# Result stores of the routed last layer, issued inside the loop over block quads

## The chip, the cores and the metric

The kernel runs on one core of a Trainium2 chip. The metric is the device time of one launch in microseconds. The kernel before took 2792.13 us, the median of three runs (2788.15 to 2796.69).

## What is computed

Four layers on x of shape 4 x 2048 x 256, each added to x after a layer norm: a linear attention with random features, a soft mixture of experts, a causal attention with rotary positions, and a mixture of 32 experts with the two best experts for each token. The change lies in the last layer:

```python
x = x + _L1_attn_ref(...)
x = x + _L1_ffn_ref(_layernorm(x, axis=-1), router_w, expert_weights)

# _L1_ffn_ref
logits = einsum('bsh,eh->bse', x, router_w)
rw = softmax(logits).reshape(T, E)
vals, idx = top_k(rw, 2)
w_masked = zeros_like(rw).at[arange(T)[:, None], idx].set(vals)
out = sum over experts e of (x_flat * w_masked[:, e:e+1]) @ expert_weights[e]
```

## The kernel before

X holds all tokens in SBUF: 64 tiles of 128 tokens, 256 values each, 64 KB a partition. The last stage, `tail`, first finishes the attention (output projection, added to X) and finds for each token its two experts and its places in a buffer in DRAM in which the tokens lie sorted by expert (`dest`). The tiles are dealt with in three groups (`TAIL`): tiles 0 to 15, 16 to 47 and 48 to 63. Each group has its own buffer of blocks of 128 rows: 64, 96 and 64 blocks (`BLOCKS`), 224 together. A block belongs to one expert. Four blocks are a quad: 56 quads, q = 0 to 55, of which 0 to 15 belong to the first group, 16 to 39 to the second, 40 to 55 to the third. Two blocks are a pair: 112 pairs, j = 0 to 111.

For each group the steps are:

- **GpSimd** scatters the tokens of a tile to their two places, two indirect DMAs a tile (L2054).
- **SyncE** loads a quad of sorted rows into one of four buffers `xin` (`load`, L2003) and stores a quad of results from one of two buffers `yout` (`keep_y`, L2008). Its program is a list written out in order: four loads, then for each q the store of quad q and the load of quad q + 4, and after the last quad the sixteen result stores (L2015 to L2017), each of four tiles of X (512 KB, in rows of 1 KB) to the output. Store f waits for the additions of tiles 4f to 4f + 3.
- **TensorE** transposes a pair (L2366) and multiplies it by its expert's weights (L2417). It is three pairs ahead with the transposes: the first pair of quad q + 4 is transposed just ahead of the multiplication of pair 2q + 5.
- **ScalarE** copies the transposed pair (L2283) and the products into `yout` (L2290). `keep_y(q)` waits for the product of pair 2q + 1.
- **GpSimd** gathers the two result rows of each token, two indirect DMAs a tile (L2065). The first gather of a group waits until all quads of the group have landed in DRAM; every tile waits for the additions of the tile four before it, since there are four slots.
- **VectorE** adds the two weighted rows to X, two operations a tile (L2268, L2270), and raises `added`.

SyncE executes its list strictly in order, so what waits in it holds back what stands behind.

Of the kernel before, what the change touches and what calls it, by code (L numbers as in the profile page):

```python
# [15 lines left out]
NT = B * TPB  # L16
# [1876 lines left out]
def tail(nc, mem, io, keep, st):  # L1893

    X, mean, rstd, ident = keep["X"], keep["mean"], keep["rstd"], keep["ident"]
# [45 lines left out]
    xc_ready, multiplied, y_ready, restored, added, stored = (mem.sem(n) for n in (  # L1941
        "xc_ready", "multiplied", "y_ready", "restored", "added", "stored"))
# [18 lines left out]
    ov = io["out"].rearrange("b (q n p) d -> (b q) p n d", n=4, p=P)  # L1961
# [7 lines left out]
    def wait_sent(eng, g):  # L1969

        t0, tiles = TAIL[g]
        for s in range(NO):
            eng.wait_ge(sent[s], 32 * len(range(s, t0 + tiles, NO)))

    with nc.Block() as block:
        @block.sync
        def _(sp):
            sp.sem_inc(a_loaded[0], 16)
            for c in range(1, NT // 4):
                if c >= 2:  # L1980
                    sp.wait_ge(projected, 2 * (c - 2) + 2)
                if c == NT // 4 - 1:
                    sp.wait_ge(last_stored, 64)
                sp.dma_start(ay[c % 2][:, :, :], ao[c // 4, :, c % 4 * 512:(c % 4 + 1) * 512].rearrange("(c p) n -> p c n", p=P)).then_inc(a_loaded[c % 2], 16)
                if c >= 1:
                    for a in range(DC):
                        e = slice(2 * c - 2, 2 * c)
                        sp.dma_start(W[:, a, e, :], io["we"][e, a * P:(a + 1) * P, :].rearrange("e p d -> p e d")).then_inc(w_loaded, 16)
                if c == 2:
                    sp.wait_ge(last_divided, 1)  # L1990
                    for h in range(4):
                        sp.dma_start(keep["ao"][B * G - 1, h, :, 3 * 512:4 * 512],
                                     keep["aT1"][32 * h + h % 2 * HD:32 * h + h % 2 * HD + HD, :]).then_inc(last_stored, 16)
            for a in range(DC):
                sp.dma_start(W[:, a, 30:32, :], io["we"][30:32, a * P:(a + 1) * P, :].rearrange("e p d -> p e d")).then_inc(w_loaded, 16)

            def load(q):
                g = group_of[q * NB]
                if q * NB == base[g]:
                    wait_sent(sp, g)  # L2000
                if q >= NX:
                    sp.wait_ge(turned, NP + (q - NX + 1) * NB // 2)
                sp.dma_start(xin[q % NX][:, :, :], xgv[g][q - base[g] // NB]).then_inc(x_in[q % NX], 16)  # L2003

            def keep_y(q):
                g = group_of[q * NB]
                sp.wait_ge(y_ready, (q + 1) * NB // 2)
                sp.dma_start(ygv[g][q - base[g] // NB], yout[q % NY][:, :, :]).then_inc(y_out[q % NY], 16)  # L2008
            for q in range(NX):
                load(q)  # L2010
            for q in range(NQ):
                keep_y(q)
                if q + NX < NQ:
                    load(q + NX)
            for q in range(NT // 4):  # L2015
                sp.wait_ge(added, q * 4 + 4)
                sp.dma_start(ov[q], X[:, q * 4:q * 4 + 4, :]).then_inc(stored, 16)  # L2017
            sp.wait_ge(stored, 16 * (NT // 4))

        @block.gpsimd  # L2020
# [252 lines left out]
        def _(act):  # L2273
# [32 lines left out]
            def restore(t):  # L2306
                for g, (t0, _) in enumerate(TAIL):
                    if t == t0:
                        wait_sent(act, g)
                s.activation(X[:, t, :], X[:, t, :], ACT.Identity, bias=mean[:, t:t + 1]).then_inc(restored, 1)  # L2310
# [233 lines left out]
```

## Time and profile before

| what | value |
|---|---|
| median of three runs | 2792.13 us |
| the profiled execution's own time | 2787.93 us |
| its span, first to last instruction | 2786.1 us |
| PE, ACT, DVE, POOL busy | 89%, 64%, 56%, 26% |
| mean granted TensorE clock | 0.956 of full speed |
| DMA traffic over the span | 308.9 MB, mean 111 GB/s |

The profile covers one execution. Its span is 1.8 us shorter than its own time, and its own time is 4.2 us below the median, within the spread of the three runs. The shares are means over all stages; the change touches the last 155 us alone, where the loop over quads ends at 2734 us and the last gathers and stores end at 2786 us.

### The profile page before, as it was taken

What the parts mean: (1) busy time and instruction counts of PE and PEld (TensorE: products, weight loads), DVE (VectorE), ACT (ScalarE), POOL (GpSimd) and SP (SyncE); (2) the same over time, 40 slices, a digit from 0 to 9 for tenths busy, and PEclk for the clock granted to TensorE, in tenths of its full rate; (3) what the DMA queues carried; (4) which work ended last, traced back from release to release, by engine and by line L of the source; (5) the groups of instructions that cost most, each with busy time, mean ns of one, the idle gap of its engine ahead of it and who ended that gap; (6) DMA issues with size and microseconds to landing.
All of it is one profiled execution on the core that took longest, in us unless ns stands there. A gap on an engine that the chain in (4) does not pass through costs nothing. (4 is left out here: it accounts for less than half of the span.)

```text
span 2786.1 us, 64193 instructions
## 1 busy us (share of the span) xinstructions
PE 2475.4 (89%) x25127; PEld 1442.7 (52%) x25131; DVE 1569.5 (56%) x2607; ACT 1793.5 (64%) x2682; POOL 736.8 (26%) x1006
## 2 busy tenths in 40 slices
PE   7888888887788989987999999999999998897992
PEld 4555555554677766653334333333333337776771
DVE  4767768577766557755554445555454437840223
ACT  3443535344455434546999999999999992465540
POOL 3203021030000016861211122221211120475566
PEclk9999999999899999988999999999999999899996
DMA  7800000000200004474766756666766605587887
GB/s 252 287 32 2 1 1 1 1 1 1 48 1 1 1 12 147 138 164 114 127 124 114 123 105 105 120 127 116 119 122 117 113 10 154 173 289 244 279 291 258
DMA packets 252048, 308.90 MB, mean 111 GB/s; under 512 B 100592, under 2 KB 180208, under 8 KB 251632
## 3 DMA queue, kind: packets, MB, share of 16 engines
q1 hardware_dynamic: 237392, 269.49, 41.0%
q0 software_dynamic: 12288, 33.57, 3.4%
q8 instruction: 200, 3.28, 0.5%
q10 hardware_dynamic: 2080, 1.84, 0.2%
q14 instruction: 88, 0.72, 0.1%
HBM read 157.23 MB, written 147.59 MB: 109 GB/s over the span
## 5 line engine op out<-in xcount | busy, mean ns | idle before, releaser
L1816 ACT ACTIVATE at_PT<-at_pS 128x1024 f32<-128x1024 f32 (+2 forms) x1152 | 1002.3, 1256 | 9.1 <-PE at_pS L1843 8.9
L1670 POOL TENSOR_SCALAR_AFFINE_SELECT at_PT<-at_PT 128x256 f32<-128x256 f32 (+1 forms) x384 | 197.5, 523 | 820.3 <-ACT at_PT L1816 819.8
L1843 PE MATMUL at_pS<-hd_QT,hd_KT 99*32 99x512 bf16 (+3 forms) x5120 | 316.9, 351 | 7.8 <-DVE at_QT L1788 5.1
L1843 PE MATMUL at_pS<-at_QT,at_KT 99*32 99x512 bf16 (+3 forms) x5120 | 318.1, 348 | 2.2 <-issue 0.7
L1767 DVE COPY md_y<-at_pO 128x512 f32<-128x512 f32 x64 | 44.2, 691 | 474.7 <-PE at_pO L1861 469.9
L1861 PE MATMUL at_pO<-at_PT,at_V 128*32 128x512 f32 (+3 forms) x2560 | 289.7, 529 | 0.3 <-POOL at_PT L1670 0.3
L1861 PE MATMUL at_pO<-at_PT,hd_V 128*32 128x512 f32 (+3 forms) x2560 | 286.8, 529 | 0.6 <-issue 0.6
L1843 PEld LDWEIGHTS at_pS<-hd_QT,hd_KT 99*32 99x32 bf16 x5120 | 111.4, 95 | 268.8 <-ACT at_PT L1816 174.1
L1843 PEld LDWEIGHTS at_pS<-at_QT,at_KT 99*32 99x32 bf16 x5120 | 114.6, 95 | 257.3 <-ACT at_PT L1816 169.0
L457 ACT ACTIVATE la_ft<-la_ft 128x1024 f32<-128x1024 f32 x128 | 135.2, 1056 | 161.5 <-DVE la_ft L280 161.2
L2417 PE MATMUL tl_bank<-tl_W,tl_xT 128*128 x896 | 225.6, 390 | 14.5 <-issue 13.3
L273 DVE TENSOR_REDUCE la_mx<-la_pW 128x16 f32<-128x1024 f32 x128 | 155.0, 1211 | 87.5 <-PE la_pW L571 87.5
L514 POOL TENSOR_SCALAR la_ft<-la_ft 128x1024 f32<-128x1024 f32 x64 | 66.8, 1045 | 465.2 <-ACT la_ft L457 465.2
L2417 PEld LDWEIGHTS tl_bank<-tl_W,tl_xT 128*128 128x128 f32 x896 | 156.8, 191 | 55.4 <-issue 40.2
L1336 POOL TENSOR_TENSOR qk_rqk<-qk_xc,qk_xs 128x256 f32<-128x256 f32 x64 | 54.1, 845 | 470.7 <-DVE qk_xs L1262 463.7
L2054 POOL DMA_INDIRECT rows_in<-all_X,all_dest x128 | 123.9, 968 | 165.0 <-DVE all_dest L2205 90.8
L280 DVE TENSOR_TENSOR la_ft<-la_pW,la_mx 128x1024 f32<-128x1024 f32 x128 | 156.8, 1225 | 10.0 <-issue 0.5
L2283 ACT ACTIVATE tl_xT<-tl_bank 128x512 f32<-128x512 f32 x144 | 85.1, 591 | 102.7 <-PE tl_bank L2366 102.3
L1437 PE MATMUL qk_pQK<-fr_W,qk_zT 128*128 128x512 f32 x256 | 128.2, 625 | 18.4 <-ACT qk_zT L1373 18.4
L553 PE MATMUL la_R<-la_zT,la_qkv_w 128*128 128x512 f32 x256 | 124.4, 632 | 21.7 <-ACT la_zT L406 21.7
L2268 DVE SCALAR_TENSOR_TENSOR all_X<-md_ay,all_wt,all_X 128x256 f32<-128x256 f32 x32 | 15.6, 486 | 181.3 <-DMA md_ay<-rows_out,all_dest 181.0
L1593 DVE RECIPROCAL md_y<-md_y 128x512 f32<-128x512 f32 x32 | 107.3, 3353 | 2.7 <-issue 0.4
(376 smaller groups left out, 4297.1 us busy)
## 6 DMA issues: line engine op xcount, KB each, us to landing
tl_xin<-rows_in SPq DMA_DIRECT2D x56, 512.0 KB, 5.6
score_terms<-at_parts SPq DMA_DIRECT2D x60, 384.0 KB, 6.2
rows_in<-la_zeros SPq DMA_DIRECT2D x8, 2048.0 KB, 7.9
rotated_qk<-qk_qkT SPq DMA_DIRECT2D x16, 1024.0 KB, 4.5
at_qk<-rotated_qk SPq DMA_DIRECT2D x60, 256.0 KB, 4.3
rows_out<-md_y SPq DMA_DIRECT2D x28, 512.0 KB
rows_out<-tl_yout SPq DMA_DIRECT2D x28, 512.0 KB, 3.8
rows_in<-la_zeros SPq DMA_DIRECT2D x4, 3072.0 KB, 10.8
```

What stands on the lines that cost most here:

```text
L273: v.tensor_reduce(mx[s % 2][:, :], src, AX, ALU.max)
L280: v.tensor_tensor(ft[s % 4][:, :].rearrange("p (h m) -> p h m", h=H), src, mx[s % 2][:, :].unsqueeze(2).broadcast_to([P, H, M]), ALU.subtr ...
L457: sc.activation(ft[s % 4][:, :], ft[s % 4][:, :], ACT.Exp, scale=0.25).then_inc(exp_done, 1)
L553: last = mm(out[:, :], W[:, a, col:col + P], zT[:, a, :], start=(a == 0), stop=(a == DC - 1))
L1437: last = mm(pQK[f % 2][:, :], zT[f][:, c, :], W[:, c, 0:2 * D], start=(c == 0), stop=(c == DC - 1))
L1593: v.reciprocal(out[:, :], out[:, :])
L1670: nc.gpsimd.affine_select(out=d, in_=d, compare_op=ALU.is_ge, fill=0.0, base=0, pattern=of, channel_multiplier=-1).then_inc(masked, 1)
L1816: nc.scalar.activation(PT[u % 6][:, 0:banks, 0:width], pS[u % 3][:, 0:banks, 0:width], ACT.Exp, scale=HD ** -0.5).then_inc(exp_done, 1)
L1843: last = mm(pS[u % 3][r:r + 32, b, col:col + 512 - off], KT[par][0:KS, h, kb * P + r:kb * P + r + 32], QT[par][0:KS, h, c * 512 + off:(c + ...
L1861: last = mm(pO[c % 2][32 * h:32 * h + 32, off:512], V[par][:, kb, VCOL[h]:VCOL[h] + 32], PT[u % 6][:, b, col:col + 512 - off], start=(kb = ...
L2054: g_.indirect_dma_start(out=keep["xg"][g], out_offset=bass.IndirectOffsetOnAxis(ap=dest[:, k, t:t + 1], axis=0), in_=X[:, t, :], in_offset ...
L2417: last = mm(pP[j % 3][:, w * D:(w + 1) * D].unsqueeze(1), xT[(NP + j) % 4][:, w, a, :], W[:, a, ds(e, 1), :], start=(a == 0), stop=(a == D ...
```

## The change

The last loop is split. The stores of tiles 0 to 43 (f = 0 to 10) are issued within the loop over quads, one at every second quad from q = 35 to q = 55, behind `keep_y(q)` and `load(q + 4)`; f = 11 to 15 follow after the loop. Every store keeps its wait. Nothing else is changed: the other engines' instructions are the same.

```diff
+            def store(f):
+                sp.wait_ge(added, f * 4 + 4)
+                sp.dma_start(ov[f], X[:, f * 4:f * 4 + 4, :]).then_inc(stored, 16)
             for q in range(NQ):
                 keep_y(q)
                 if q + NX < NQ:
                     load(q + NX)
-            for q in range(NT // 4):
-                sp.wait_ge(added, q * 4 + 4)
-                sp.dma_start(ov[q], X[:, q * 4:q * 4 + 4, :]).then_inc(stored, 16)
+                if q >= 35 and (q - 35) % 2 == 0:
+                    store((q - 35) // 2)
+            for f in range(11, NT // 4):
+                store(f)
             sp.wait_ge(stored, 16 * (NT // 4))
```

The list of SyncE, first at quads 35 to 37, before. `rows_out` is the store of a quad (from `tl_yout` for odd q, from `md_y` for even q), `tl_xin` the load four quads ahead, `out_dram` a result store.

```order
 L2008 DMA rows_out<-tl_yout 128x1024
 L2003 DMA tl_xin<-rows_in 128x1024
-L2008 DMA rows_out<-md_y 128x1024
-L2003 DMA tl_xin<-rows_in 128x1024
-L2008 DMA rows_out<-tl_yout 128x1024
-L2003 DMA tl_xin<-rows_in 128x1024
```

And with the change, at the same place:

```order
+L2014 DMA out_dram<-all_X 128x4x256
+L2008 DMA rows_out<-md_y 128x1024
+L2003 DMA tl_xin<-rows_in 128x1024
+L2008 DMA rows_out<-tl_yout 128x1024
+L2003 DMA tl_xin<-rows_in 128x1024
+L2014 DMA out_dram<-all_X 128x4x256
```

A result store now stands behind the load of each odd quad, ahead of the next even quad's store and load.

The end of SyncE's list, from quad 51 on. Before, the four last quad stores and then all sixteen result stores:

```order
-L2008 DMA rows_out<-md_y 128x1024
-L2008 DMA rows_out<-tl_yout 128x1024
-L2008 DMA rows_out<-md_y 128x1024
-L2008 DMA rows_out<-tl_yout 128x1024
-L2017 DMA out_dram<-all_X 128x4x256 x16
```

With the change:

```order
+L2014 DMA out_dram<-all_X 128x4x256
+L2008 DMA rows_out<-md_y 128x1024
+L2008 DMA rows_out<-tl_yout 128x1024
+L2014 DMA out_dram<-all_X 128x4x256
+L2008 DMA rows_out<-md_y 128x1024
+L2008 DMA rows_out<-tl_yout 128x1024
+L2014 DMA out_dram<-all_X 128x4x256 x6
```

Eight result stores stand ahead of quad 51's store, one each behind quads 51 and 53, and six (f = 10 to 15) behind quad 55.

## Rows read from the trace of the kernel before

**Rows 1.** Chain that ended last, 2630 us to the end: start us, us, what.

```profile
2668.80 6.63 DMA tl_xin<-rows_in
...
2675.48 0.66 PE tl_bank L2366 x4
2676.13 0.46 issue
2676.59 2.02 PE tl_bank L2417 x8
...
2679.05 1.73 PE tl_bank L2417 x8
...
2683.96 6.85 DMA tl_xin<-rows_in
...
2715.43 6.15 DMA tl_xin<-rows_in
...
2778.58 2.72 DMA tl_ay<-rows_out,all_dest
```

**Rows 2.** GpSimd in order of time, the gathers (idle before, and what ended it).

```profile
2656.48 0.94 POOL L2065 DMA_INDIRECT md_ay<-rows_out,all_dest  x1 [25.35 <-DMA rows_out<-tl_yout]
...
2738.14 0.95 POOL L2065 DMA_INDIRECT md_ay<-rows_out,all_dest  x1 [0.30 <-issue]
...
2760.83 0.94 POOL L2065 DMA_INDIRECT md_ay<-rows_out,all_dest  x1 [1.16 <-issue]
...
2778.58 0.94 POOL L2065 DMA_INDIRECT tl_ay<-rows_out,all_dest  x1 [0.30 <-issue]
```

**Rows 3.** SyncE's queue in order of time: quads 39, 53, 55, and the sixteen stores.

```profile
2652.91 0.32 SPq L2008 DMA_DIRECT2D rows_out<-tl_yout  x1
...
2725.44 0.32 SPq L2008 DMA_DIRECT2D rows_out<-tl_yout  x1
...
2734.28 0.32 SPq L2008 DMA_DIRECT2D rows_out<-tl_yout  x1
2734.65 48.54 SPq L2017 DMA_DIRECT2D out_dram<-all_X  x16
```

**Rows 4.** VectorE in order of time: second additions of tiles 39 and 63.

```profile
2722.59 0.48 DVE L2270 SCALAR_TENSOR_TENSOR all_X<-tl_ay,all_wt,all_X 128x256 f32<-128x256 f32 x1
...
2782.30 0.48 DVE L2270 SCALAR_TENSOR_TENSOR all_X<-tl_ay,all_wt,all_X 128x256 f32<-128x256 f32 x1 [0.43 <-issue]
```

**Rows 5.** Stretches: busy time by engine; last: TensorE clock, DMA share, GB/s.

```profile
2634.00:2664.00 30.00, 28.18 (x146) 22.45 (x145) 2.00 (x4) 13.24 (x24) 5.69 (x7) 1.00 0.68 237
2664.00:2724.00 60.00, 54.27 (x279) 42.92 (x278) 22.91 (x48) 25.51 (x46) 45.88 (x47) 1.00 0.89 305
...
2744.00:2754.00 10.00, 0.00 (x0) 0.00 (x0) 3.01 (x7) 0.00 (x0) 7.55 (x9) 0.50 1.06 385
```

**Rows 6.** L2003, loads issued 2640 to 2720 us (quads 36 to 51).

```profile
L2003 SPq DMA_DIRECT2D tl_xin<-rows_in x16: 320/432/1252, 2640.0 to 2715.4; - x16
...
DMA to landing us min/median/max: 4.1/5.6/6.6
```

**Rows 7.** The load issued at quad 48, alone.

```profile
L2003 SPq DMA_DIRECT2D tl_xin<-rows_in x1: 436/436/436, 2699.8 to 2699.8; - x1
...
DMA to landing us min/median/max: 5.9/5.9/5.9
```

**Rows 8.** L2017, the sixteen result stores: duration ns, then landing us.

```profile
L2017 SPq DMA_DIRECT2D out_dram<-all_X x16: 372/1444/2088, 2734.6 to 2782.8; - x16
...
DMA to landing us min/median/max: 2.9/7.6/9.6
```

**Rows 9.** What TensorE waited for, 2634 to 2735 us: total us, times, longest.

```profile
PE tl_bank L2417 <- issue: 6.0, 13, 0.7
PE tl_bank L2366 <- DMA tl_xin<-rows_in: 1.9, 4, 0.8
```

## The prediction

> **What bounds the kernel now.** I read the chain that ended last first, from 2630 us on, because the change touches nothing earlier. It runs through three kinds of work: TensorE's pairs, now and then a load of sorted rows that TensorE waited for, and from the last quad store on GpSimd's gathers [rows 1]. The reader is to see that no result store is in it except the very last. Then GpSimd's order of time [rows 2]. Its gathers for tiles 16 to 63 start at 2656.48 us, when quad 39 has landed in DRAM, and go on almost without a gap to 2778.58 us: 96 gathers of some 1.25 us each (0.94 busy, 0.30 between). The third group's 32 gathers may start when quad 55 has landed. So two things hold the end at once: GpSimd's own pitch from 2656.48 us on, and the quad store issued at 2734.28 us [rows 3]. How close the second is: quad 39's store was issued at 2652.91 us and GpSimd started 3.57 us later; the same 3.57 us behind 2734.28 us is 2737.85 us, and GpSimd came to the third group at 2738.14 us. The slack is 0.3 us. Whatever delays the product of quad 55 by more than that delays the end one for one.
>
> **What the burst at the end costs now.** The sixteen result stores stand from 2734.65 us to 2783.2 us in SyncE's queue [rows 3]. The first eleven are ready when the loop ends (their tiles' additions are done), and they fill the DMA engines: 385 GB/s and a share of 1.06 from 2744 to 2754 us [rows 5], 1.44 us of the queue for each and 7.6 us to landing in the median [rows 8]. But the last store waits for the additions of tile 63, which end at 2782.78 us [rows 4], and lands 2.9 us behind its issue [rows 8], long after the burst is gone. The burst can cost only what it does to the gathers beside it: the 32 gathers of the third group are issued over 41.4 us (2738.14 to 2779.52) where 32 at 1.25 us would take 40.0; one gap of 1.16 us instead of 0.30 stands at 2760.83 us [rows 2].
>
> **The change, part by part.**
>
> *Eleven stores leave the end.* Of those 1.4 us I take the one gap, 1.16 - 0.30 = 0.9 us, as the gain, since gathers that take over 1 us are found elsewhere too. Bounds: a gain of 1.4 us and, if the gap has another cause, 0. The last five stores stay as they are; f = 10 stays right behind quad 55, where the burst began already.
>
> *Eleven waits on `added` enter SyncE's list.* Behind each are the next quad's store and load. The first four (tiles 0 to 15) were added before 2638 us and wait for nothing later than that. From f = 4 on the additions run close ahead of the quads. The smallest slack of these is that of f = 9: tile 39 is done at 2723.07 us, and SyncE is through with the store of quad 53 at 2725.76 us, 2.7 us later [rows 3, 4]. A wait that overran would hold back nothing at once, since the next quad's store comes 5.09 us after this one (16 quads from 2652.91 to 2734.28 us [rows 3]). So additions have to be later by 6 us and more before this wait costs. I cost it at nothing; the cover is the pace of GpSimd, which the change leaves.
>
> *Eleven transfers of 512 KB enter the loop.* This is the term that decides. A store stands behind the load of its odd quad in the same queue, so the next even quad's store and load start behind it. Per quad the loop now moves 0.52 MB of products, 0.52 MB of sorted rows and some 0.53 MB of gathers (305 GB/s times 5.09 us is 1.55 MB in all) [rows 5]. At the highest rate that the trace shows, 385 GB/s, this takes 4.0 us of the 5.09 us, so 1.1 us is free; one store more takes 0.52 MB / 385 GB/s = 1.4 us, with the gathers that go on beside it 1.8 us. The backlog that meets the next load is between 1.4 - 1.1 = 0.3 and 1.8 - 1.1 = 0.7 us. I take 0.7 us, since rate and share are at their ceiling for a whole quad only in the burst.
>
> Which loads does it meet? Those issued at quads 36 to 50, even ones. In the stretch up to 2664 us there are hardly gathers, 237 GB/s in the mean [rows 5], and the free time covers the store: 0 for f = 0 and 1, so quad 39 and GpSimd's start at 2656.48 us stay. There remain the six loads issued at quads 40, 42, 44, 46, 48 and 50. How late may a load be? The sixteen loads of quads 36 to 51 take 5.6 us in the median, 4.1 at least [rows 6]; those that the chain passes through landed after 6.63, 6.85 and 6.15 us [rows 1], while one of 5.9 us is not in it [rows 7]. I put the limit at 6.0 us. One of the six, of 6.63 us (quad 42), is over it already and passes on the whole 0.7 us; quad 40's meets few gathers and passes on nothing; I take four at the median, which go from 5.6 to 6.3 us, 0.3 over the limit each: 0.7 + 4 x 0.3 = 1.9 us. A TensorE that waited for its rows starts again slowly: 0.46 us of issue and 2.02 instead of 1.73 us for the next eight multiplications [rows 1], 0.75 us. Four loads would newly do that, 3.0 us; but 13 such pauses, 6.0 us, are there already against only four waits for loads [rows 9], so a new one will often stand in for an old one. I take half, 1.5 us (0 and 3.0 us stay as bounds). Sum: TensorE ends 1.9 + 1.5 = 3.4 us later.
>
> *Sum.* 3.4 - 0.3 (slack of quad 55) - 0.9 (burst) = +2.2 us on 2787.93 us, the profiled execution's own time: 2790.1 us. The runs' median is 4.2 us above that execution; the same 2.2 us on 2792.13 us gives **2794.3 us**. Measurements of this kernel tell some 0.3%, 8.4 us, from no change, so this is "same".
>
> *The upper end.* If each of the six loads is later by what one more store costs the queue in the burst, 1.44 us [rows 8], five at the median go to 7.0 us, 1.0 over the limit each, and quad 42's passes on 1.4: 6.4 us, with five restarts 3.8 us; no gain from the burst: 6.4 + 3.8 - 0.3 = +9.9 us, 2802 us.
>
> **The rivals.**
>
> *A, hidden altogether.* The backlog drains in the 5 us between quads, or the late loads fall together with pauses that are there. Then GpSimd's pitch alone sets the end and the burst's share is won: -0.9, at best -1.4 us, 2791 us. For it: TensorE waited only 1.9 us for loads in 100 us [rows 9]. Against it: the loads that it did wait for make up the chain [rows 1].
>
> *B, slower.* The DMA engines are full in the loop, the queue doesn't drain between one store and the next, and the backlog grows from quad to quad. Place: the ten loads issued at quads 42 to 51. Price: if they take what the stores of the burst took, 7.6 us [rows 8], each is 1.6 us over the limit; 1.6 us of that is there already (0.6, 0.85 and 0.15 us), so 16 - 1.6 = 14.4 us, and seven new restarts of 0.75 us, 5.3 us: +19 us, 2811 us. It decides from where the traffic asked for reaches the ceiling. Asked for from 2664 to 2724 us are 305 GB/s x 60 us = 18.3 MB and six stores, 3.1 MB: 21.4 MB or 357 GB/s. Against it: 385 GB/s are shown, 7% more [rows 5]. For it: that rate was reached with a full queue, in which each transfer waits long.
> The Trainium skill's page "DMA: Bandwidth & Descriptors", section "Where 436 GB/s comes from", speaks for this rival: it says that transfers between HBM and SBUF are bound on the HBM side at about 358 GB/s a core. By that ceiling the loop would be exactly full and rival B would be the likeliest. The trace's 385 GB/s over 10 us disagrees with it on this chip, so I leave B as a rival.
>
> *C, SyncE is held by a store's wait.* Gathers delayed by the traffic push the additions 6 us back (slack 2.7 us plus most of a quad), the quad store behind comes late, and with it the end. Gathers would have to take over 10 us, none here is near that. If it came, each us past the 6 would cost 1 us: 2796 to 2803 us.
>
> *D, faster by over 0.3%.* I find no mechanism, since the gathers' own pitch holds from 2656.48 us on, and the stores cost at most 1.4 us. Only the spread of the medians could show it.
>
> **How the numbers follow.** My forecast (a net slip of 0 to 8 us) 0.57; A 0.25; B 0.08; C 0.02; the remainder, a slip of 8 to 12 us by larger backlogs than I take, 0.03; D 0.05. The three runs before spread by -4.0 and +4.6 us around their median. The range takes A less most of that spread, 2791 - 4, and goes up to the upper end of the forecast: 2787 to 2802 us. Faster 0.05, same 0.82, slower 0.13.
>
> **What would show it.** In the changed kernel's profile: result stores of the loop issued without idle time ahead of the next quad store; loads issued at even quads from 42 on landing 0.3 to 0.7 us later than those at odd ones, 6 us and more; TensorE's wait for loads from 2634 us up from 1.9 us to 3 or 4 us; quad 55's store at 2736 to 2739 us instead of 2734.28; and the first gather of the third group waiting for `rows_out`. The gap ahead of the gather at 2760 us gone, and 385 GB/s found nowhere for long. I am wrong if quad 55's store is where it was (A), if loads take over 7 us at odd quads too (B), or if SyncE waits for VectorE between quads (C).

## The result and the profile after

The changed kernel takes 2801.41 us (median of nine runs, 2798.57 to 2808.07), the kernel before, on the same chip, 2792.11 us (nine runs). The ratio is 1.0037, with a 95% interval of 1.0025 to 1.0048: 9.3 us slower. Forecast was no change, +2.2 us.

The profiled execution has a span of 2799.8 us, 13.7 us above that of the profile before. That is more than the 9.3 us between the medians, because the execution profiled before lay 4.2 us below its median and this one at its median. Where the 13.7 us come from is read from SyncE's queue and GpSimd. SyncE's queue in order of time (start us, us, engine line op), around quads 39, 43 and 55:

```profile
2657.56 0.32 SPq L2008 DMA_DIRECT2D rows_out<-tl_yout  x1
...
2680.81 0.32 SPq L2008 DMA_DIRECT2D rows_out<-tl_yout  x1
2681.17 0.43 SPq L2003 DMA_DIRECT2D tl_xin<-rows_in  x1
2681.65 0.77 SPq L2014 DMA_DIRECT2D out_dram<-all_X  x1
2687.37 0.32 SPq L2008 DMA_DIRECT2D rows_out<-md_y  x1
...
2692.33 0.32 SPq L2008 DMA_DIRECT2D rows_out<-tl_yout  x1
...
2749.78 0.32 SPq L2008 DMA_DIRECT2D rows_out<-tl_yout  x1
```

Quad 35's store is at 2635.80 us (2633.53 us before): these 2.3 us arose before the first early store, so the change did not make them. From quad 35 to quad 55 the loop takes 113.98 us, before it took 100.75 us: **+13.2 us**. And the time goes in one place: from an odd quad's store to the next even one's it is now 6.5 us in the median (6.56 us above, 2680.81 to 2687.37), from an even one's to the next odd one's 5.0 us (4.96 us above). Before, they were 5.0 and 4.9 us. The early store stands in the long interval.

GpSimd, start of the second and of the third group:

```profile
2661.26 0.95 POOL L2070 DMA_INDIRECT md_ay<-rows_out,all_dest  x1 [28.16 <-DMA rows_out<-tl_yout]
...
2753.18 0.94 POOL L2070 DMA_INDIRECT md_ay<-rows_out,all_dest  x1 [10.30 <-issue]
```

The third group starts at 2753.18 us, after 10.3 us without work, 3.4 us behind quad 55's store. Before, GpSimd came to it without a wait [rows 2]. From there to the end it is 46.6 us (2753.18 to 2799.8), before 48.0 us: the burst at the end had cost 1.3 us. So 2.3 + 13.2 - 0.5 (slack and landing of quad 55: GpSimd started 3.9 us behind that store before, 3.4 us now) - 1.3 = 13.7 us.

What TensorE waited for between the stores of quads 35 and 55 (us in total, times, longest):

```profile
PE tl_bank L2422 <- issue: 17.7, 25, 1.2
PE tl_bank L2371 <- DMA tl_xin<-rows_in: 1.2, 2, 0.8
```

The stretches that answer to [rows 5] (last: TensorE clock, DMA share, GB/s):

```profile
2634.00:2664.00 30.00, 25.46 (x129) 20.15 (x130) 0.97 (x2) 11.38 (x21) 2.13 (x3) 1.00 0.78 256
2664.00:2724.00 60.00, 48.94 (x242) 38.50 (x242) 20.86 (x44) 22.25 (x42) 45.68 (x48) 0.97 0.96 321
```

The DMA engines carry 321 instead of 305 GB/s, and TensorE is busy for 48.9 instead of 54.3 us of the 60. The waits answer to [rows 9]. The waits for loads, on which the forecast rested, went down from 1.9 to 1.2 us. What grew, by 11.7 us, are the pauses ahead of multiplications in which the engine waits for nothing that the profile shows. These pauses are the greater part of the 13.2 us, but not all of it. The same 463 instructions of TensorE between the stores of quads 35 and 55 are also busy for longer, before and with the change:

```profile
2633.53:2734.28 100.75, 91.98 (x463) 72.09 (x462) 28.91 (x60) 42.69 (x77) 59.24 (x61) 1.00 0.80 275
2635.80:2749.78 113.98, 94.36 (x463) 73.54 (x462) 31.58 (x66) 42.36 (x77) 62.44 (x64) 0.99 0.87 291
```

TensorE's idle time grew by 10.9 us (the 11.7 us of pauses, less what the waits for loads fell) and its busy time by 2.4 us. A part of the latter goes with the clock: the granted clock was 0.90 from 2717 to 2722 us, where the engine was busy for 2.9 of 5 us in a wait for rows and two pauses, and 0.76 in the next 5 us; in the profile before it was 1.00 in both. TensorE's order of time behind the store of quad 43 shows where they stand:

```profile
2682.15 0.60 PE L2371 MATMUL tl_bank<-all_ident,tl_xin 128*128 128x128 f32 x4
2683.24 1.13 PE L2422 MATMUL tl_bank<-tl_W,tl_xT 128*128 x4 [0.48 <-issue]
2685.59 1.13 PE L2422 MATMUL tl_bank<-tl_W,tl_xT 128*128 x4 [1.23 <-issue]
2686.55 0.60 PE L2371 MATMUL tl_bank<-all_ident,tl_xin 128*128 128x128 f32 x4
```

A pause ahead of the first four multiplications of a pair, and one in its middle, ahead of the second four. Nothing changes hands in the middle of a pair: both blocks' rows and the result's bank are ready. But there is one instruction there that is no matrix work. `multiply` reads each block's expert from SBUF into a register (`pe.value_load(which[...])`), once ahead of every four multiplications, since the address of the weights depends on it. All 25 pauses stand ahead of such a group of multiplications. That became the theory.

A rival would be that TensorE waited for its own program to be fetched. The traces speak against it: between the stores of quads 35 and 55 the DMA queues marked "instruction" carry 9 packets before and 9 with the change, while the pauses go from 13 to 25, more than one for each packet.

### The profile page after: what moved, and what is told of

Read it like the earlier page. It is cut to its first block and busy times, and to the rows that moved or that the text cites. A ratio compares the mean times of both kernels' runs of the same rounds, so it can differ in the third digit from the quotient of the medians.

```text
span 2799.8 us, 64193 instructions
## 1 busy us (share of the span) xinstructions
PE 2474.7 (88%) x25127; PEld 1444.0 (52%) x25131; DVE 1570.8 (56%) x2607; ACT 1792.9 (64%) x2682; POOL 737.4 (26%) x1006
```

## The experiments

**Theory R**: the pauses are these register loads, which take longer while the DMA engines carry the early store. **Theory L**, the prediction's: sorted rows land late.

The runs came to several chips, and these are of two kinds. Chips of kind A run the kernel before in 2790 to 2792 us: that of the result and those numbered 3 and 9. Chips of kind B take 2838 to 2844 us: those numbered 6, 7 and 11. "Chip A" and "chip B" stand for a chip of the kind in what follows. A profile of the kernel before on chip B (before_again) shows the added time in the loop over quads: 344.8 us from quad 0 to quad 55, on chip A 290.3 us, part of it in stalls in which TensorE advances by one or two instructions with some 2 us between them. Why was not found. Ratios are to runs of the kernel before on the same chip, and can differ by up to 3 us from the quotient of the two medians shown. Two versions that ran on different chips are compared by their ratios, which is weaker than a comparison on one chip.

| run | chip | median us | before us | ratio, 95% interval | pauses behind odd quads | behind even quads |
|---|---|---|---|---|---|---|
| before (profile) | A | | | | 2.4 us | 2.9 us |
| changed | A | 2801.41 | 2792.11 | 1.0037 [1.0025, 1.0048] | 12.3 | 2.1 |
| even_too | A 3 | 2807.21 | 2790.45 | 1.0060 [1.0045, 1.0075] | 11.2 | 3.3 |
| even_only | A 9 | 2797.21 | 2791.14 | 1.0018 [1.0005, 1.0032] | 2.3 | 8.8 |
| sbuf_all | A 3 | 2802.47 | 2790.45 | 1.0052 [1.0034, 1.0069] | 7.5 | 2.4 |
| even_const | A 3 | 2783.81 | 2790.45 | 0.9976 [0.9964, 0.9987] | 0 | 0 |
| multi8_after | A 3 | 2782.24 | 2790.45 | 0.9973 [0.9961, 0.9985] | 0 | 0 |
| multi8_before_again | A 9 | 2783.26 | 2791.14 | 0.9966 [0.9951, 0.9981] | 0 | 0 |
| before_again (one run) | B 11 | 2845.18 | 2843.89 | | 3.1 | 3.2 |
| after_again | B 11 | 2848.14 | 2843.89 | 1.0013 [1.0001, 1.0024] | 7.5 | 4.9 |
| const_before | B 6 | 2823.59 | 2838.30 | 0.9946 [0.9930, 0.9962] | 0.3 | 0 |
| const_after | B 6 | 2825.31 | 2838.30 | 0.9945 [0.9925, 0.9965] | 0 | 0 |
| rows_4k | B 6 | 2841.66 | 2838.30 | 1.0012 [1.0000, 1.0025] | 8.7 | 3.6 |
| extra_loads | B 6 | 2842.53 | 2838.30 | 1.0012 [1.0002, 1.0021] | 4.7 | 1.7 |
| sbuf_copy | B 7 | 2844.26 | 2843.38 | 1.0003 [0.9989, 1.0016] | 3.4 | 4.7 |
| dram_copy | B 7 | 2842.87 | 2843.38 | 1.0001 [0.9990, 1.0012] | 5.0 | 2.1 |
| part16 | B 7 | 2843.00 | 2843.38 | 1.0003 [0.9990, 1.0016] | 6.0 | 4.6 |
| multi4_before | B 11 | 2831.40 | 2843.89 | 0.9965 [0.9952, 0.9978] | 0 | 0 |
| multi4_after | B 11 | 2835.47 | 2843.89 | 0.9972 [0.9963, 0.9982] | 0 | 0 |
| multi8_before | B 7 | 2833.43 | 2843.38 | 0.9962 [0.9950, 0.9975] | 0.8 | 0 |

The last two columns are sums over one profiled execution: TensorE's pauses ("issue") ahead of multiplications of the loop, in the nine intervals from an odd quad's store (35 to 53) to the next even one's and in the eight from an even one's (36 to 52) to the next odd one's, quads 41 to 43 left out in all of them because of chip B's stall there. One execution each, so differences of a few us between such sums are not told from chance; even_only's profile is of one of its slowest executions (2803.98 us, its median is 2797.21 us).

**Without the register loads.** Both kernels with the experts as constants. The blocks are multiplied by other experts' weights than they should be, so the result is not that of the layer; the work is the same.

```diff
-                    e = pe.value_load(which[0:1, 2 * j + w:2 * j + w + 1], min_val=0, max_val=E1 - 1)
+                    e = (2 * j + w) % E1
...
-                        last = mm(pP[j % 3][:, w * D:(w + 1) * D].unsqueeze(1), xT[(NP + j) % 4][:, w, a, :], W[:, a, ds(e, 1), :], start=(a == 0), stop=(a == DC - 1))
+                        last = mm(pP[j % 3][:, w * D:(w + 1) * D].unsqueeze(1), xT[(NP + j) % 4][:, w, a, :], W[:, a, e:e + 1, :], start=(a == 0), stop=(a == DC - 1))
```

const_before: 

> The kernel before, with the expert of each block written into TensorE's program as a constant (block number modulo 32) instead of read from SBUF into a register by an instruction of TensorE; the products are those of other experts, the work is the same. Theory R (TensorE's pauses, called issue in its waits, are its register loads from SBUF, which take longer while DMA engines read SBUF): the pauses between the multiplications, 2.3 + 3.3 + 1.3 + 4.7 = 11.6 us from 2521 to 2734 us, go to under 3 us, and the whole is 4 to 8 us faster than before. Theory L (the prediction's: loads of sorted rows land too late): pauses stay within 1 us of 11.6 us, time within 2 us of before.

const_after: 

> The changed kernel with the same constants in place of the register loads. Theory R: the pauses from 2634 us on, 17.6 us in the changed kernel, go to under 4 us, and the time is within 3 us of const_before, where the changed kernel is 9.3 us above the kernel before. Theory L: the difference to const_before stays 8 to 11 us, with the waits for tl_xin making it up.

Waits of TensorE between the stores of quads 35 and 55, const_before:

```profile
PE tl_bank L2366 <- DMA tl_xin<-rows_in: 12.7, 8, 3.5
PE tl_bank L2366 <- issue: 8.4, 5, 2.3
...
PE tl_bank L2417 <- issue: 1.5, 2, 1.2
```

and the same of the kernel before on that chip:

```profile
PE tl_bank L2417 <- issue: 17.0, 16, 4.0
PE tl_bank L2366 <- DMA tl_xin<-rows_in: 8.0, 4, 3.1
```

The pauses ahead of multiplications are gone, 16 of them become 2, and in const_after there is none. What is left of chip B's stall now stands ahead of transposes (L2366, 8.4 us; 13.5 us in 7 places in const_after). The time is 15 us below before, and the changed kernel and the kernel before have the same ratio. Theory L's mark, 8 to 11 us between the two, is missed. The gain is larger than expected (4 to 8 us). On this chip alone the second half says less than it seems, because the change costs little there:

> The changed kernel once more, on the chip of this call. Theory R and theory L: 1.002 to 1.005 times before, as on the first chip. If it is within 0.15% of before here, the loss of the change depends on the chip and the four experiments of the second chip have to be read by their pauses, not by their times.

> The kernel before once more, for a profile on the chip of this call: the chip of the first four experiments ran it in 2838.3 us, 46 us above the first chip. Both theories: the time of its own runs; the pauses of TensorE from quad 35 to quad 55 and its waits for rows on this chip are the base for the three runs beside it.

after_again is 1.0013: the loss is 4 us on chip B, 9 us on chip A, just below the range expected. The pauses behind odd quads rise there too, from 3.1 to 7.5 us, but so much else stalls that less of it reaches the end. From here on the pauses are read as well as the times.

**Stores at other places.** even_too adds ten stores behind the loads of the even quads, to a scratch tensor; even_only moves the early stores there; even_const is even_too with constants.

```diff
                 if q >= 35 and (q - 35) % 2 == 0:
                     store((q - 35) // 2)
+                elif 35 < q < 55:
+                    again((q - 36) // 2)
```

even_too: 

> The changed kernel with ten more stores of the same size and shape, to a scratch tensor in DRAM, one behind the load of each even quad from 36 to 54: the suspected cost doubled, at places that have none now. Theory R: the pauses ahead of the multiplications between an even quad's store and the next odd one's rise from 2 to 5 us to 7 to 12 us, as they stand behind the odd quads in the changed kernel (12.3 us on the first chip, 7.5 us on the second, quads 41 to 43 left out), and the time is 4 to 9 us above the changed kernel's. Theory L: the pauses behind even quads stay, and waits for tl_xin grow to 10 us and more.

even_only: 

> The changed kernel with its early stores behind the even quads 36 to 54 instead of the odd ones 35 to 55 (f = 0 to 9; f = 10 goes to the end). Ten stores behind even quads beside eleven behind odd ones gave 3.3 us of pauses behind even and 11.2 us behind odd quads. If what counts is that a store stands in a quad, whichever: 7 to 13 us of pauses behind even quads, 2 to 4 us behind odd ones, 1.003 to 1.004 times before on the first chip. If the parity matters: under 5 us behind both, within 0.15% of before.

even_const: 

> even_too with constants in place of the register loads. If the added traffic of 21 stores costs only by way of the register loads, no pauses and within 3 us of const_after, 0.9945 times before. Theory L: loads land late under 21 stores, 5 us and more above const_after.

even_only's waits between quads 35 and 55:

```profile
PE tl_bank L2422 <- issue: 14.6, 19, 1.3
PE tl_bank L2371 <- DMA tl_xin<-rows_in: 2.2, 3, 1.2
```

In even_only the pauses move with the stores: 8.8 us behind even quads, 2.3 us behind odd ones, and the intervals turn round (6.9 us behind even, 5.0 us behind odd, medians). The time, 1.0018, lies between the two marks. even_too costs 7.5 us more than the changed kernel, as expected, but its pauses behind even quads are only 3.3 us: there the expectation failed. With stores in every quad the pauses become more frequent (33 against 25) and shorter, and stay largest behind odd quads. Their sum between quads 35 and 55 does not grow at all: 17.9 us against 17.7 us. The stretch is still 5.5 us longer than in the changed kernel, and all of that is in TensorE's busy time:

```profile
2636.34:2755.77 119.43, 99.84 (x463) 74.49 (x462) 32.31 (x68) 42.47 (x77) 62.51 (x64) 0.97 0.94 324
```

These are 99.8 us for the instructions that took 94.4 us with eleven stores and 92.0 us without, at a granted clock of 0.97 instead of 0.99 and 1.00. So the sum of pauses is not the whole cost of the stores. How much of this is the clock and how much is delay too short to show as a pause was not separated. Why the pauses stay behind odd quads is open; even_only excludes that an even quad as such is harmless.

even_const shows on chip A what many stores cost without register loads. It carries 21 stores in the loop. The stretch from 2660 to 2720 us (last: TensorE clock, DMA share, GB/s) and the waits between quads 35 and 55:

```profile
2660.00:2720.00 60.00, 51.07 (x264) 42.28 (x263) 22.83 (x47) 24.95 (x44) 45.46 (x47) 0.97 1.03 387
```

```profile
PE tl_bank L2378 <- DMA tl_xin<-rows_in: 10.0, 11, 2.5
```

At 387 GB/s over 60 us loads do land late, for 10.0 us in all, as theory L said of such traffic. But these waits fill time that the register loads had taken: the stretch from quad 35 to 55 takes 100.3 us, as in the kernel before (100.75 us) and 19.1 us less than in even_too, and the whole is 6.6 us faster than before. There is no pause, as expected. The ratio of 0.9976 is not the expected one, though: it was to be within 3 us of const_after, 0.9945, and by the ratios it is 9 us above, in the range that theory L gave. The two numbers are from chips of different kinds, and on chip A the two other versions without pauses, with few register loads (below), stand at 0.9966 and 0.9973 too, so that the mark says little; constants without early stores were not run on chip A. What speaks against theory L there is the changed kernel itself, in which TensorE waited 1.2 us for rows. The changed kernel has half as many stores; its traffic does not set the end by itself.

**What the register load is sensitive to.** Five runs put other transfers where the early stores stand: rows_4k (the stores in rows of 4 KB, to a scratch tensor), extra_loads (DRAM to SBUF), dram_copy (DRAM to DRAM), sbuf_copy and sbuf_all (SBUF to SBUF, 11 and 21 of them), and part16 leaves partitions 0 to 15 to the end. extra_loads and the copies keep all sixteen result stores behind the loop. The diff shows the one transfer of each run, shortened; its waits are left out.

```diff
-                sp.dma_start(ov[f], X[:, f * 4:f * 4 + 4, :]).then_inc(stored, 16)
+                sp.dma_start(keep["v4k"][f].rearrange("p (n d) -> p n d", n=4), X[:, f * 4:f * 4 + 4, :]).then_inc(stored, 16)   # rows_4k
+                sp.dma_start(st4, io["x"].rearrange("b (q n p) d -> (b q) p n d", n=4, p=P)[f]).then_inc(filled, 16)   # extra_loads
+                sp.dma_start(keep["v1k"][f], xs[f]).then_inc(filled, 16)   # dram_copy, xs: the input in the same shape
+                sp.dma_start(st4, X[:, f * 4:f * 4 + 4, :]).then_inc(filled, 16)   # sbuf_copy, sbuf_all
+                sp.dma_start(ov[f][16:P], X[16:P, f * 4:f * 4 + 4, :]).then_inc(stored, 16)   # part16
```

rows_4k: 

> The changed kernel, but the eleven early stores go to a scratch tensor in DRAM in rows of 4 KB (128 of them) instead of to the output in rows of 1 KB (512); tiles 0 to 43 are missing in the output. Same bytes, a quarter of the rows. If the number of rows delays TensorE: 3 us and less above before. If the bytes do (read from SBUF, or traffic as such): 8 to 11 us above before, as the changed kernel.

extra_loads: 

> The kernel before, all sixteen result stores at the end as there, and at the places where the change puts its eleven stores eleven loads of the same size and shape (512 KB, rows of 1 KB) from the input x into a scratch tile of SBUF that nobody reads. It tells whether the direction counts. Theory R in its narrow form (reading SBUF by DMA is what delays the register load): within 2 us of before, pauses from 2634 us on 6 to 8 us. Theory R in its wide form (any added traffic or descriptors) and theory L: 8 to 11 us slower than before.

sbuf_copy: 

> At the places of the eleven early stores, with the same waits, eleven copies of the same tiles of X into a scratch tile of SBUF; all sixteen result stores are at the end as before. SBUF is read as by the change, DRAM is not touched. If reading SBUF by DMA is what delays the register loads: 23 to 30 pauses of TensorE ahead of its multiplications from quad 35 to quad 55, as in the changed kernel (25 on the first chip, 28 on the second; 13 and 16 without the change), and 3 to 11 us above before. If writing DRAM is: 13 to 18 pauses and within 3 us of before.

dram_copy: 

> At the same places, with the same waits, eleven copies of 512 KB in rows of 1 KB from the input in DRAM to a scratch tensor in DRAM, SBUF not touched; all sixteen result stores at the end. If reading SBUF delays the register loads: 13 to 18 pauses from quad 35 to 55, within 3 us of before. If any added traffic or the writes to DRAM do: 23 and more pauses and 4 to 11 us above before.

sbuf_all: 

> All sixteen result stores at the end, and behind every quad from 35 to 55 a copy of four tiles of X into a scratch tile of SBUF: 21 copies. Eleven such copies left the pauses behind odd quads at 3.4 us, against 3.1 us without and 7.5 us with the stores. If that was chance and reading SBUF is what counts: 7 us and more behind odd and behind even quads, 4 to 10 us above before. If only a store from SBUF to DRAM counts: 3 to 5 us behind each, within 3 us of before.

part16: 

> The changed kernel with the early stores of partitions 16 to 127 only; the rows of partitions 0 to 15 of tiles 0 to 43 are stored at the end by two transfers. Same result. The register that TensorE loads lies in partition 0. If the delay comes from the engines or the port that serve the first partitions: 13 to 18 pauses from quad 35 to 55 and within 2 us of before or faster. If any reading of SBUF delays it: 23 and more pauses, and the time of the changed kernel, 1.0013 to 1.0037 times before.

With a quarter of the rows (rows_4k) the pauses behind odd quads are as in after_again, 8.7 against 7.5 us, and so is the time, 1.0012 against 1.0013: nothing shows that the number of rows counts. Loads into SBUF and copies within DRAM raise the pauses from 3.1 us to 4.7 and 5.0 us, which one execution each doesn't tell from chance. The time of extra_loads, 1.0012, is as high as with the stores; that of dram_copy, 1.0001, is not, though writing DRAM or any traffic was to cost 4 to 11 us. So the direction of a transfer is not singled out. Eleven copies within SBUF (sbuf_copy) left the pauses at 3.4 us and the time at 1.0003, against the theory that reading SBUF is enough. But 21 of them on chip A (sbuf_all) cost 12 us, where 4 to 10 us were expected, with 28 pauses in 12.4 us between quads 35 and 55, against 13 in 6.0 us [rows 9]. Behind odd quads these are 7.5 us, as expected, behind even ones only 2.4 us, where 7 us and more were expected. SyncE waited 36.2 us for copies to land, each ahead of the next copy, but it was not late by that: it still waited for ScalarE ahead of the quad stores. As in even_too, a part of the cost is busy time, 96.9 us in place of 92.0 us, here at a granted clock of 1.00. So traffic that reads and writes SBUF alone, without any write to DRAM, can bring out such pauses; that reading is what does it is not shown. part16 left 6.0 us of pauses and no loss of time (1.0003) on chip B, where the loss is 4 us; whether partition 0 matters is undecided. Counted from quad 35 to 55, dram_copy and sbuf_copy have 21 pauses each, between the marks of both readings (13 to 18, and 23 and more), and part16 has 27.

**Fewer register loads.** One load of four or of eight values in place of four or eight loads:

```diff
+                if 2 * j % 8 == 0:
+                    experts[:] = nc.values_load_multi_w_load_instructions(which[0:1, 2 * j:2 * j + 8], engines=(mybir.EngineType.PE,), min_val=0, max_val=E1 - 1,
+                        skip_runtime_bounds_check_because="the experts are 0 to 31")[1]
                 for w in range(2):
-                    e = pe.value_load(which[0:1, 2 * j + w:2 * j + w + 1], min_val=0, max_val=E1 - 1)
+                    e = experts[2 * j % 8 + w]
```

multi4_before: 

> The kernel before with one register load of four values for each quad, ahead of the quad's first pair, in place of four loads of one value, one ahead of each block. Same result. Theory R: three of four places of a pause are gone; the sum of TensorE's pauses between quads 0 and 55 falls from 13.3 us to 3 to 8 us, and the time is 3 to 8 us below before. Theory L: no change beyond 2 us.

multi4_after: 

> The changed kernel with one register load of four values for each quad. Theory R: most of the loss of the change goes, since the quad's register load is issued at the even pair, some 2 us behind the odd quad's store, and is one instead of two beside the store: within 4 us of multi4_before. Theory L: 8 to 11 us above multi4_before.

multi8_before: 

> The kernel before with one register load of eight values for every two quads. Same result. Theory R: 13 to 16 us below before on the second chip (four values: 12.5 us, constants: 14.7 us), 5 to 11 us on the first. It is the version meant to beat both kernels.

multi8_after: 

> The changed kernel with one register load of eight values for every two quads. Theory R: as multi8_before within 3 us, 0.996 to 0.997 times before.

multi8_before_again: 

> The kernel before with one register load of eight values for every two quads, for the chip of this call. If it is the first chip's kind: multi8_after was 0.9973 times before there, and GpSimd's pitch sets the end in both, so 0.996 to 0.999, the two within 3 us.

On chip B four values give 12.5 us by the medians, more than the 3 to 8 expected; eight give 10 us there, where 13 to 16 were expected, and 7.9 us on chip A, as expected. By the ratios four and eight are alike on chip B, 10 and 11 us. multi8_after, with the early stores, is 8.2 us faster than before on chip A and within 1 us of multi8_before_again (2 us above it by the ratios, whose intervals overlap): with few register loads **no cost of the early stores is seen in the time** there, and both versions beat both kernels. On chip B multi4_after is still 4 us above multi4_before, at the edge of what was expected, with intervals that overlap.

The edit does more than group the loads. It also skips the check that the value is within its bounds. The profiles count 64193 instructions in the kernel before, 63577 in multi4_before and 63549 in multi8_after: of the 616 and 644 that are gone, 168 and 196 are the loads saved, and the other 448 are two for each of the 224 blocks. The constants take both away as well. So what is shown is that a register load together with its check costs the pauses; the load alone was not tested. Waits between quads 35 and 55, and GpSimd at the start of the third group, of multi8_after:

```profile
PE tl_bank L2371 <- DMA tl_xin<-rows_in: 8.7, 9, 1.6
```

```profile
2727.25 1.21 POOL L2070 DMA_INDIRECT md_ay<-rows_out,all_dest  x1 [0.30 <-issue]
```

No pause is left, and waits for rows take part of the room. They show what the stores do cost TensorE once the pauses are gone: from quad 35 to 55 it takes 96.8 us in multi8_after and 93.1 us in multi8_before_again, 3.7 us more, with 8.7 and 6.2 us of waits for rows (one execution each). That fits theory L's mechanism, and the 3.4 us that the forecast took for it. It does not reach the end, because quad 55's store is out at 2718.82 us, 8.4 us before GpSimd comes to the third group: the gathers' pitch alone sets the end. GpSimd comes to that group without a wait in multi8_before_again too, so from quad 39 on nothing more is to be won there by a faster TensorE.

## Why the prediction was wrong

- **What holds the end**: right. GpSimd waited for quad 55, and the slack was 0.3 us, so TensorE's delay came through nearly whole. Put at nothing, though, was any delay up to quad 39: there TensorE's pauses are 3.0 us in place of 0.3 us, the stretch from quad 35 to 39 is 2.4 us longer, and GpSimd started its gathers at 2661.26 instead of 2656.48 us (2.3 of these 4.8 us arose before the first early store).
- **The burst at the end**: right; 1.3 us where 0.9 us was taken, with 1.4 us as the bound.
- **The waits on `added`**: right; SyncE waited for VectorE once between quads 35 and 55, 0.6 us.
- **The eleven transfers in the loop**: wrong, and this is the step that failed. It was priced as loads landing 0.7 us later at even quads, 6.3 us and more. The ones issued at the even quads 40 to 48 land after 5.6 to 5.9 us, that of quad 50 after 4.7 us, in the median of all sixteen 5.8 instead of 5.6 us [rows 6], and TensorE waited less for them than before. The price was in the other row of [rows 9]: 6.0 us of pauses in 13 places. I took these for the restarts of a TensorE that had waited for rows, and let new ones stand in for old. But 13 pauses stood against four waits, so at least nine had no wait ahead of them, and some stood in the middle of a pair, as this one, which follows four multiplications directly:

```profile
2660.19 1.03 PE L2417 MATMUL tl_bank<-tl_W,tl_xT 128*128 x4
2661.61 1.13 PE L2417 MATMUL tl_bank<-tl_W,tl_xT 128*128 x4 [0.40 <-issue]
```

They were register loads, with their checks, that the work queued ahead did not quite cover, and with the transfers beside them they are more and longer: 17.7 us in 25 places. The term was 3.4 us; it measured 13.2 us, within 0.2 us 11.7 us of it by these pauses and 2.4 us by longer busy time, less 0.7 us of waits for rows. Late loads as they were priced appear only where the register loads are gone or grouped: in multi8_after as some 3.7 us of TensorE's time that do not reach the end.
- **Rival B**: wrong in its mechanism, though right in its sign; no load issued at an odd quad took over 7.0 us. even_const moves 387 GB/s over 60 us, so 357 GB/s was not the ceiling. The Trainium skill's limit of about 358 GB/s on the HBM side, page "DMA: Bandwidth & Descriptors", section "Where 436 GB/s comes from", is exceeded by this trace as well, for traffic all of which has a side in HBM.
- **Rivals A and C**: wrong; quad 55's store came 13.2 us later, measured from quad 35, and SyncE's waits had no part in it.
- The range held the time, but that was luck: its upper end, +9.9 us, was worked out from late loads and restarts behind them, and the 9.3 us came by another way. The chance of 0.13 for slower was too small.

## What to carry to other kernels

Before transfers are moved beside an engine's work, look at that engine's pauses that the profile puts down to nothing, and ask which instruction stands there in the source: a register loaded from SBUF ahead of every four multiplications was here a latency that added DMA traffic lengthened, although the loads of data landed on time. Group such loads (one for eight values instead of eight, without the check of each) before anything else is moved. The sum of the pauses is a lower bound of what they cost: look at the busy time of the same instructions too. And a store burst at the end costs only what it takes from the work that ends last, here 1.3 us.

## What was not expected of the hardware

A register load by TensorE, with its check, is dear under DMA traffic. Without early stores the pauses ahead of multiplications are 13.3 us in the loop over 56 quads on chip A, 29.4 us on chip B (there with the stall); with the change on chip A the longest single one was 1.2 us. What in the traffic lengthens them stays open. One load of four values brings the sum between quads 35 and 55 on chip B from 17.0 to 10.1 us, all of it in that chip's stall at quad 42. The same kernel, 1.7% or so apart on chips of the two kinds, lost 9 us by this change on the one and 4 us on the other.
